# The start of a one-core transformer layer on Trainium2: x on two DMA queues, split first weights, a shared norm, zero-tile matmuls, and the first key begun from x's high parts

## The chip, the core and the metric

The kernel runs on one NeuronCore of a Trainium2 chip. The metric is the device time of one execution in microseconds (us); lower is better. Engine names are those of the profile: PE (TensorE, its matmuls; PEld is its weight load), DVE (VectorE), ACT (ScalarE), POOL (GpSimd), SP (SyncE, which here only starts DMAs).

## What is computed

x has 4 sequences of 256 tokens, 256 features each, in float32. One layer is applied:

```python
x = x + attn(layernorm(x), wq, wk, wv, wo)
x = x + ffn(layernorm(x), W1, W2, W3)
```

The attention has 16 query heads and 4 key/value heads of 128 features, rotary embedding (rope) on queries and keys, and no softmax: the scores are multiplied by a causal decay table of the head. The feed-forward part is `silu(x W1) * (x W3)`, a Walsh-Hadamard transform, and a product with W2.

## The kernel before, in words

**Float32 by three products.** Every operand of a matmul is split into a high part (a copy rounded to the matmul format, made by ACT) and a low part (operand minus high part, made by DVE or POOL). `product` (L272 to L276) issues high x high, high x low and low x high into one PSUM bank. So each operand goes through ACT first, then through DVE or POOL, and then PE may use it.

**Order of the work.** The tokens are done in two halves of 512 (4 tiles of 128 tokens). Each engine has its own hand-written list, and semaphores tie the lists together. `START` (L70) is the first stretch: `X` items transpose the normalised x (two, one for each 128 features), `K`, `Q` and `V` items are projections of 128 columns (K, Q: one head) or of one token tile (V). `LIN` and `LIN_NO` number all such items, `lin_bank` gives their PSUM bank. Then come 16 units `u` (a half and a pair of heads each): `scores` in three parts (`S_FIRST0`, `S_SECOND`, `S_FIRST1`), the decay `mask` by DVE, `high_p` by ACT, `low_p` by DVE, `attend`, `high_o`, `low_o`, `project_out`. Queries and keys are projected two units ahead (`queries`, `key`).

**The first stretch before.** SP loads x of the first half (L246, two DMAs of 256 KB), then three weight chunks of 512 KB (L242): chunk 0 is wk, 1 is the first quarter of wq, 2 is wv, 3 the second quarter of wq, 4 the first of wo. ACT's own queue brings the identity and the rope tables (L561 to L563). There are 3 slots in `w_raw`, so chunk n waits for the low part of chunk n-3. DVE computes the norm's statistics (L724 to L731), POOL the inverse deviation (L640), DVE the normalised x (L748). PE transposes it (L287, eight transposes into banks 0 and 1), ACT takes the high parts (L486), DVE the low ones (L760). Then PE projects K, Q, V, Q, V, ...

**Rope.** For a K or Q item ACT copies the two halves of the bank crosswise into `rope_b` (`swap`, L509 and L510), DVE multiplies by the tables (`rotate`, L779 and L780), POOL adds (`rope_add`, L647), ACT takes the high part (`high_rope`, L515) and POOL the low part (`low_rope`, L654). Two buffers alternate. The first key and the four first queries are called K0, Q0 to Q3 below, the value items V0 to V3, the next queries Q4 and Q5; the second key, K1, is made during unit 1.

**Weights.** `high_weights` (ACT, L481) and `low_weights` (DVE, L754, for chunks 0 to 3; POOL, L659, from chunk 4 on) split a chunk. DVE's list has the low part of chunk 3 after V0 (L865); ACT's list has the high part of chunk 3 before the first `swap` (L569). Unit 0 needs chunk 3 for Q4 and Q5.

**What ends the first stretch on ACT** (L581 to L586): `high_v` of V3, `high_rope` of Q2, `high_p` of the first scores, `high_rope` of Q3, `high_p` of the second scores, `high_weights(4)`, and then unit 0 with the swaps of Q4 and Q5.

Of the kernel before, what the change touches and what calls it, by code (L numbers as in the profile page):

```python
# [57 lines left out]
CHUNKS = [("wk", 0, AT_K), ("wq", 0, AT_Q), ("wv", 0, AT_V), ("wq", 1, AT_Q + CH), ("wo", 0, AT_O),  # L58
# [7 lines left out]
LOW_ON_DVE = 4  # L66
# [3 lines left out]
START = ([("X", 0, k) for k in range(KD)] + [("K", 0, 0), ("Q", 0, 0), ("V", 0, 0), ("Q", 0, 1), ("V", 0, 1),  # L70
          ("Q", 0, 2), ("V", 0, 2), ("Q", 0, 3), ("V", 0, 3)])
# [48 lines left out]
def build(nc, x, wk, wv, wq, wo, w1, w3, w2, cos, sin, decay, ident, hadamard, out):  # L120
    dram = {"wk": wk, "wv": wv, "wq": wq, "wo": wo, "w1": w1, "w3": w3, "w2": w2}

    with ExitStack() as ctx:
# [55 lines left out]
        tables_loaded = sem("tables_loaded")  # L179
# [3 lines left out]
        stored = sem("stored")  # L183
# [5 lines left out]
        half_set, rstd_done, xn_done = sem("half_set"), sem("rstd_done"), sem("xn_done")  # L189
# [47 lines left out]
        def _(sp):  # L237
            def load_chunk(n):
                if n >= SLOTS:
                    wait_low_weights(sp, n - SLOTS)  # L240
                w, i, _ = CHUNKS[n]
                sp.dma_start(w_raw[:, n % SLOTS, :], dram[w][i]).then_inc(w_loaded[n % SLOTS], 16)  # L242

            def load_x(c):
                for i in range(BH * c, BH * (c + 1)):
                    sp.dma_start(x_sb[:, 2 * i:2 * i + 2, :], x[i]).then_inc(x_loaded[i], 16)  # L246
# [5 lines left out]
            for n in range(3):  # L252
                load_chunk(n)
# [4 lines left out]
            load_x(1)  # L258
# [12 lines left out]
        def _(pe):  # L271
# [21 lines left out]
            def project(item):  # L293
# [180 lines left out]
        def _(act):  # L474
            def high_weights(n):
                _, _, at = CHUNKS[n]
                act.wait_ge(w_loaded[n % SLOTS], 16 * (n // SLOTS + 1))
# [159 lines left out]
        def _(pool):  # L637
# [50 lines left out]
            low_rope(("Q", 0, 1))  # L688
            rope_add(("Q", 0, 2))
# [4 lines left out]
            for u in range(UNITS):  # L694
# [12 lines left out]
                if unit_chunk(u) is not None:  # L707
# [7 lines left out]
        def _(dve):  # L715
# [271 lines left out]
```

## Time and profile before

| | |
|---|---|
| median of 3 runs | 277.31 us (277.09, 277.31, 278.17) |
| the profiled execution's own time | 277.34 us |
| its span in the profile | 275.5 us |
| PE busy | 257.6 us (93% of the span) |
| PEld, DVE, ACT, POOL busy | 82%, 75%, 61%, 56% |

The page's second part cuts the span into 40 slices of 6.9 us:

```profile
PE   0796878999999999999999999999999999999995
DVE  2878799899997988967999898795756985144433
ACT  2586787678689767655667777995352552043230
POOL 1049989978878935813597787899709400000000
```

Each digit is the busy share of a slice in tenths. PE is at 9 from the eighth slice on; the first seven slices, up to 48 us, are where it is not.

### The profile page before, as it was taken

To read this page: it belongs to the slowest core of one execution; us is meant where nothing else is said; L and a number is where in the kernel's file an instruction comes from. 1 tells how busy PE (TensorE), PEld (TensorE's weight loads), DVE (VectorE), ACT (ScalarE), POOL (GpSimd) and SP (SyncE) were. 2 spreads that over 40 slices of the span, in tenths; PEclk is the share of its full clock that TensorE was granted. 3 is DMA by queue.
4 is the path that set the end of the run, shared out by engine and by line. 5 is a ranking of instruction groups with operands and counts; after the bars stand their busy time and mean duration, and the time that the engine had idled before them with its cause. 6 is when DMAs were issued, how large, how long until landed. Compare 5 with 4: busy or idle time off the path is not lost.

```text
span 275.5 us, 4150 instructions
## 1 busy us (share of the span) xinstructions
PE 257.6 (93%) x1480; PEld 225.1 (82%) x1480; DVE 206.1 (75%) x324; ACT 167.1 (61%) x279; POOL 153.2 (56%) x111
## 2 busy tenths in 40 slices
PE   0796878999999999999999999999999999999995
PEld 0584766898898988878888888898989879988895
DVE  2878799899997988967999898795756985144433
ACT  2586787678689767655667777995352552043230
POOL 1049989978878935813597787899709400000000
PEclk9999999999999999999999999999999999999999
DMA  7695022102022000000002002200000000200002
GB/s 259 242 355 190 0 80 77 59 20 76 4 76 76 0 2 0 1 4 0 0 2 76 2 0 76 76 4 1 2 0 0 2 0 0 79 0 0 2 0 76
DMA packets 5203, 13.23 MB, mean 48 GB/s; under 512 B 576, under 2 KB 2112, under 8 KB 5184
## 3 DMA queue, kind: packets, MB, share of 16 engines
q1 hardware_dynamic: 4752, 12.65, 13.0%
q10 hardware_dynamic: 432, 0.33, 0.4%
q8 instruction: 12, 0.20, 0.3%
q14 instruction: 7, 0.06, 0.1%
HBM read 11.93 MB, written 1.05 MB: 47 GB/s over the span
## 4 chain that ended last, share of the span: by engine, by line
PE 70%; DVE 13%; POOL 5%; issue 5%; ACT 3%; DMA 3%; SPq 0%; DVEq 0%; POOLq 0%
PE bank L274 24%; PE bank L275 23%; PE bank L276 23%; DVE rope_b L780 3%; POOL qk L647 2%; POOL q_hid L654 2%; DVE rope_a L779 2%; DMA w_raw<-in_wq 1%; DMA x_sb<-in_x 1%; PE bank L287 1%; DVE xn L748 1%; DVE rope_b L817 1%; DVE w_lo L754 1%; POOL w_lo L659 1%; DVE p_lo L798 1%
## 5 line engine op out<-in xcount | busy, mean ns | idle before, releaser
L647 POOL TENSOR_TENSOR qk<-rope_a,rope_b 128x512 f32<-128x512 f32 x40 | 53.5, 1341 | 34.8 <-DVE rope_b L780 34.4
L274 PE MATMUL bank<-xt_hi,w_hi 128*128 128x512 f32 x144 | 57.4, 398 | 1.5 <-DVE rope_a L779 0.8
L275 PE MATMUL bank<-xt_lo,w_hi 128*128 128x512 f32 x144 | 56.9, 395 | 0.0
L276 PE MATMUL bank<-xt_hi,w_lo 128*128 128x512 f32 x144 | 56.6, 393 | 0.0
L654 POOL TENSOR_TENSOR q_hid<-qk,q_hid 128x512 fp32r<-128x512 f32 x32 | 43.0, 1355 | 9.7 <-ACT q_hid L515 9.7
L780 DVE TENSOR_TENSOR rope_b<-rope_b,sin_sb 128x512 f32<-128x512 f32 x40 | 42.1, 1053 | 0.0
L522 ACT ACTIVATE p_hi<-bank 128x512 fp32r<-128x512 f32 x48 | 28.6, 596 | 15.7 <-DVE bank L793 15.2
L779 DVE TENSOR_TENSOR rope_a<-bank,cos_sb 128x512 f32<-128x512 f32 x40 | 27.5, 686 | 14.2 <-ACT rope_b L510 13.5
L275 PE MATMUL bank<-w_lo,o_hi 128*128 128x256 f32 x128 | 36.2, 283 | 0.0
L276 PE MATMUL bank<-w_hi,o_lo 128*128 128x256 f32 x128 | 36.2, 283 | 0.0
L274 PE MATMUL bank<-w_hi,o_hi 128*128 128x256 f32 x128 | 36.1, 282 | 0.0
L274 PEld LDWEIGHTS bank<-xt_hi,w_hi 128*128 128x128 f32 x144 | 27.6, 191 | 8.0 <-DVE rope_a L779 1.0
L798 DVE TENSOR_TENSOR p_lo<-bank,p_hi 128x512 fp32r<-128x512 f32 x48 | 32.7, 680 | 1.4 <-ACT p_hi L522 1.0
L276 PEld LDWEIGHTS bank<-xt_hi,w_lo 128*128 128x128 f32 x144 | 27.5, 191 | 5.9
L793 DVE TENSOR_TENSOR bank<-bank,decay_sb 128x512 f32<-128x512 f32 x48 | 32.0, 688 | 0.5
L275 PEld LDWEIGHTS bank<-xt_lo,w_hi 128*128 128x128 f32 x144 | 27.5, 191 | 5.1
L509 ACT ACTIVATE rope_b<-bank 64x512 f32<-64x512 f32 x40 | 23.8, 596 | 11.8 <-PE bank L276 11.0
L533 ACT ACTIVATE rope_a<-bank 128x512 f32<-128x512 f32 x16 | 9.5, 596 | 28.5 <-PE bank L276 28.5
L803 DVE TENSOR_TENSOR o_lo<-bank,o_hi 128x512 fp32r<-128x512 f32 x32 | 22.0, 687 | 5.9 <-ACT o_hi L526 5.4
L817 DVE TENSOR_TENSOR rope_b<-bank,rope_a 128x512 f32<-128x512 f32 x16 | 11.0, 689 | 20.6 <-ACT rope_a L533 20.6
L526 ACT ACTIVATE o_hi<-bank 128x512 fp32r<-128x512 f32 x32 | 19.1, 596 | 12.1 <-PE bank L276 11.4
L275 PEld LDWEIGHTS bank<-w_lo,o_hi 128*128 128x128 f32 x128 | 24.5, 191 | 0.7
(72 smaller groups left out, 591.4 us busy)
## 6 DMA issues: line engine op xcount, KB each, us to landing
w_raw<-in_w SPq DMA_DIRECT2D x6, 512.0 KB, 3.3
w_raw<-in_wq SPq DMA_DIRECT2D x4, 512.0 KB, 4.8
decay_sb<-in_decay SPq DMA_DIRECT2D x4, 512.0 KB, 6.3
w_raw<-in_wo SPq DMA_DIRECT2D x4, 512.0 KB, 3.2
x_sb<-in_x SPq DMA_DIRECT2D x4, 256.0 KB, 4.5
out<-x_sb SPq DMA_DIRECT2D x8, 128.0 KB, 1.8
w_raw<-in_wk SPq DMA_DIRECT2D x1, 512.0 KB, 4.7
w_raw<-in_wv SPq DMA_DIRECT2D x1, 512.0 KB, 6.6
```

The source lines that it names most:

```text
L274: pe.matmul(o, a_hi, b_hi, start=first, stop=False, skip_group_check=shared)
L275: pe.matmul(o, a_hi, b_lo, start=False, stop=False, skip_group_check=shared)
L276: return pe.matmul(o, a_lo, b_hi, start=False, stop=last, skip_group_check=shared)
L509: act.activation(rope_b[0:h, r % 2, :], lin_bank(n)[h:P], ACT.Copy)
L522: act.activation(p_hi[:, s, :], s_bank[s][:], ACT.Copy).then_inc(p_hi_done, 1)
L647: pool.tensor_tensor(qk[:, r % 2, :], rope_a[:, r % 2, :], rope_b[:, r % 2, :], ALU.add).then_inc(rope_sum, 1)
L654: pool.tensor_tensor(lo, qk[:, r % 2, :], hi.bitcast(F32), ALU.subtract).then_inc(rope_lo, 1)
L779: dve.tensor_tensor(a, src, c, ALU.mult).then_inc(lin_free, 1)
L780: dve.tensor_tensor(b, b, s, ALU.mult).then_inc(rope_parts, 1)
L793: dve.tensor_tensor(src, src, table, ALU.mult).then_inc(mask_done, 1)
L798: dve.tensor_tensor(p_lo[:, s, :], s_bank[s][:], p_hi[:, s, :].bitcast(F32), ALU.subtract).then_inc(p_lo_done, 1)
L803: dve.tensor_tensor(o_lo[:, b, :, :].rearrange("p h t -> p (h t)"), o_bank[:], o_hi[:, b, :, :].rearrange("p h t -> p (h t)").bitcast(F32) ...
```

## The change

Everything is in the first stretch.

- x: sequence 0 stays on SP's queue, sequence 1 goes to ACT's. The identity follows it there; the rope tables move to SP's queue behind chunk 1.
- Chunks: chunk 0 is now wv, chunk 2 is wk. The first 256 columns of wk (head K0) and the first 512 of the first wq chunk (Q0, Q1) are loaded ahead of all chunks by DMAs of their own (`load_first`), split by ACT and DVE (`high_first`, `low_first`) ahead of the rest. The rest of these chunks has 768 and 512 columns.
- Low parts: `LOW_ON_DVE = (0, 3)`; chunks 1 and 2 (their rests) go to POOL.
- Norm: DVE computes the shift, then DVE normalises tiles 0 and 1, ACT tiles 2 and 3.
- PE: 16 matmuls of a zeroed tile by itself (128x512, into bank 7) ahead of the transposes, two behind them. POOL zeroes the tile.
- K0: the four products with x's high parts go first, the two with its low parts last.
- The high part of chunk 3 moves behind V3 in ACT's list, its low part behind Q3 in DVE's list, ahead of the first two masks.

```diff
-CHUNKS = [("wk", 0, AT_K), ("wq", 0, AT_Q), ("wv", 0, AT_V), ("wq", 1, AT_Q + CH), ("wo", 0, AT_O),
+CHUNKS = [("wv", 0, AT_V), ("wq", 0, AT_Q), ("wk", 0, AT_K), ("wq", 1, AT_Q + CH), ("wo", 0, AT_O),
-LOW_ON_DVE = 4
+FIRST = ((2, 0, D), (1, 0, 2 * D))
+FIRST_OF = {n: at for n, _, at in FIRST}
+WARM_FIRST, WARM_NEXT = 16, 2
+LOW_ON_DVE = (0, 3)
@@ block.sync
+            def load_first(i):
+                n, a, b = FIRST[i]
+                w, j, _ = CHUNKS[n]
+                sp.dma_start(w_raw[:, n % SLOTS, a:b], dram[w][j][:, a:b]).then_inc(first_loaded[i], 16)
...
             load_x(0)
-            for n in range(3):
-                load_chunk(n)
+            load_first(0)
+            load_first(1)
+            load_chunk(0)
+            load_chunk(1)
+            sp.dma_start(cos_sb[:], cos).then_inc(tables_loaded, 16)
+            sp.dma_start(sin_sb[:], sin).then_inc(tables_loaded, 16)
+            load_chunk(2)
             load_chunk(3)
@@ block.tensor
+            def warm(times):
+                for _ in range(times):
+                    pe.matmul(bank[7][:], o_hi[:, 0, 0, 0:P], o_hi[:, 0, :, :], start=True, stop=True)
...
+                if item == ("K", 0, 0):
+                    for k in range(KD):
+                        pe.wait_ge(x_hi_done, k + 1)
+                        a = slice(at + k * P, at + (k + 1) * P)
+                        pe.matmul(o[:], w_hi[:, a], xt_hi[:, k, :], start=k == 0, stop=False)
+                        pe.matmul(o[:], w_lo[:, a], xt_hi[:, k, :], start=False, stop=False)
+                    for k in range(KD):
+                        pe.wait_ge(lin_free, LIN_NO[("X", c, k)] + 1)
+                        a = slice(at + k * P, at + (k + 1) * P)
+                        last = pe.matmul(o[:], w_hi[:, a], xt_lo[:, k, :], start=False, stop=k == KD - 1)
+                    last.then_inc(lin_full, 1)
+                    return
...
-            pe.wait_ge(tables_loaded, 48)
-            fill(START)
+            pe.wait_ge(zeroed, 1)
+            warm(WARM_FIRST)
+            pe.wait_ge(ident_loaded, 16)
+            fill(START[:2])
+            warm(WARM_NEXT)
+            fill(START[2:11])
             for u in range(UNITS + 1):
                 if u < UNITS:
                     scores(u, S_FIRST0)
                     scores(u, S_SECOND)
+                if u == 0:
+                    fill(START[11:])
@@ block.scalar
-            act.dma_start(ident_sb[:], ident).then_inc(tables_loaded, 16)
-            act.dma_start(cos_sb[:], cos).then_inc(tables_loaded, 16)
-            act.dma_start(sin_sb[:], sin).then_inc(tables_loaded, 16)
-            high_weights(0)
+            act.dma_start(x_sb[:, 2:4, :], x[1]).then_inc(x_loaded[1], 16)
+            act.dma_start(ident_sb[:], ident).then_inc(ident_loaded, 16)
+            norm_apply(0, range(2, TT))
+            high_first(0)
+            high_first(1)
             high_x(0, 0)
             high_x(0, 1)
+            high_weights(0)
             high_weights(1)
-            high_weights(2)
-            high_weights(3)
...
+            high_weights(2)
             high_v(0, 1)
...
             high_v(0, 3)
-            high_rope(("Q", 0, 2))
+            high_weights(3)
             high_p(0, S_FIRST0)
             high_rope(("Q", 0, 3))
@@ block.gpsimd
             pool.memset(minus_half[:], -0.5).then_inc(half_set, 1)
+            pool.memset(o_hi[:, 0, :, :].bitcast(F32), 0.0).then_inc(zeroed, 1)
             pool.wait_ge(half_set, 1)
             inverse_deviation(0)
+            low_weights(1)
             rope_add(("K", 0, 0))
...
             low_rope(("Q", 0, 1))
+            low_weights(2)
             rope_add(("Q", 0, 2))
@@ block.vector
-            norm_apply(0, range(TT))
-            low_weights(0)
+            norm_shift(0)
+            norm_apply(0, range(2))
+            low_first(0)
+            low_first(1)
             low_x(0, 0)
             low_x(0, 1)
-            low_weights(1)
-            low_weights(2)
-            dve.wait_ge(tables_loaded, 48)
-            fill(START[2:5])
+            low_weights(0)
+            dve.wait_ge(tables_loaded, 32)
+            fill(START[2:10])
             low_weights(3)
-            fill(START[5:])
             mask(0, S_FIRST0)
             mask(0, S_SECOND)
+            fill(START[10:])
```

`START` has 11 items, so PE's `START[11:]` is empty.

How the lists change at two places. First ACT, the end of the first stretch, before (`v_hid` is a value item's high part, `rope_b` a half of a swap, `q_hid` the high part of a query, `p_hi` that of masked scores, `w_hi` a chunk's):

```order
L509 ACTIVATE rope_b<-bank1 64x512
L510 ACTIVATE rope_b<-bank1 64x512
L499 ACTIVATE v_hid<-bank0 128x512
L515 ACTIVATE q_hid<-qk 128x512
L522 ACTIVATE p_hi<-bank2 128x512
L515 ACTIVATE q_hid<-qk 128x512
L522 ACTIVATE p_hi<-bank3 128x512
L481 ACTIVATE w_hi<-w_raw 128x1024
```

and in the change:

```order
L568 ACTIVATE rope_b<-bank1 64x512
L569 ACTIVATE rope_b<-bank1 64x512
L574 ACTIVATE q_hid<-qk 128x512
L558 ACTIVATE v_hid<-bank0 128x512
L539 ACTIVATE w_hi<-w_raw 128x1024
L581 ACTIVATE p_hi<-bank2 128x512
L574 ACTIVATE q_hid<-qk 128x512
L581 ACTIVATE p_hi<-bank3 128x512
L539 ACTIVATE w_hi<-w_raw 128x1024
```

The high part of chunk 3 now stands behind the high parts of Q2 and V3, and ahead of the high part of the first scores and that of Q3.

Second POOL, from the inverse deviation to chunk 4, before (`qk` is a rope sum, `k_lo` and `q_hid` are low parts, `w_lo` is the low part of a chunk):

```order
L640 TENSOR_TENSOR rstd<-var_eps,minus_half 128x4
L647 TENSOR_TENSOR qk<-rope_a,rope_b 128x512 x2
L654 TENSOR_TENSOR k_lo<-qk,k_hi 128x512
L647 TENSOR_TENSOR qk<-rope_a,rope_b 128x512
L654 TENSOR_TENSOR q_hid<-qk,q_hid 128x512 x2
L647 TENSOR_TENSOR qk<-rope_a,rope_b 128x512 x2
L654 TENSOR_TENSOR q_hid<-qk,q_hid 128x512 x2
L659 TENSOR_TENSOR w_lo<-w_raw,w_hi 128x1024
```

and in the change:

```order
L701 TENSOR_TENSOR rstd<-var_eps,minus_half 128x4
L721 TENSOR_TENSOR w_lo<-w_raw,w_hi 128x512
L708 TENSOR_TENSOR qk<-rope_a,rope_b 128x512 x2
L715 TENSOR_TENSOR k_lo<-qk,k_hi 128x512
L708 TENSOR_TENSOR qk<-rope_a,rope_b 128x512
L715 TENSOR_TENSOR q_hid<-qk,q_hid 128x512 x2
L721 TENSOR_TENSOR w_lo<-w_raw,w_hi 128x768
L708 TENSOR_TENSOR qk<-rope_a,rope_b 128x512 x2
L715 TENSOR_TENSOR q_hid<-qk,q_hid 128x512 x2
L721 TENSOR_TENSOR w_lo<-w_raw,w_hi 128x1024
```

A half chunk has come in ahead of the first rope sum, and three quarters of a chunk between the low part of Q1 and the sum of Q2.

## Rows read from the trace of the kernel before

**Rows 1.** The page: busy time of each engine.

```profile
PE 257.6 (93%) x1480; PEld 225.1 (82%) x1480; DVE 206.1 (75%) x324; ACT 167.1 (61%) x279; POOL 153.2 (56%) x111
```

**Rows 2.** Windows: length, busy us (xcount) per engine, PEclk, DMA share, GB/s.

```profile
75.00:100.00 25.00, 25.00 (x156) 22.45 (x155) 21.66 (x34) 20.87 (x37) 18.57 (x14) 1.00 0.12 43
```

**Rows 3.** PE's waits, whole span: us in total, times, longest.

```profile
PE bank L287 <- DVE xn L748: 7.7, 1, 7.7
```

**Rows 4.** Timeline of PE: start us, us, [idle before <-releaser].

```profile
11.11 0.63 PE L275 MATMUL bank<-xt_lo,w_hi 128*128 128x512 f32 x1
...
12.81 0.63 PE L276 MATMUL bank<-xt_hi,w_lo 128*128 128x512 f32 x1
...
25.73 0.50 PE L274 MATMUL bank<-w_hi,xt_hi 128*128 128x512 f32 x1 [2.28 <-DVE v_hid L766]
...
27.00 0.40 PE L276 MATMUL bank<-w_hi,xt_lo 128*128 128x512 f32 x1
...
47.59 0.50 PE L274 MATMUL bank<-q_hid,k_hi 128*128 128x512 f32 x1 [1.34 <-POOL k_lo L654]
```

**Rows 5.** Timeline of DVE and POOL up to the low part of x.

```profile
3.71 0.75 DVE L724 BATCH_NORM_STATS2 stats<-x_sb 128x6 f32<-128x256 f32 x2 [3.71 <-DMA x_sb<-in_x]
4.70 0.75 DVE L724 BATCH_NORM_STATS2 stats<-x_sb 128x6 f32<-128x256 f32 x2 [0.23 <-DMA x_sb<-in_x]
...
6.08 1.02 POOL L640 TENSOR_TENSOR rstd<-var_eps,minus_half 128x4 f32<-128x4 f32 x1 [5.25 <-DVE var_eps L731]
...
10.56 0.69 DVE L760 TENSOR_TENSOR xt_lo<-bank,xt_hi 128x512 fp32r<-128x512 f32 x1 [0.16 <-ACT xt_hi L486]
```

**Rows 6.** Line L737, the norm's shift: ns min/median/max, first and last start.

```profile
L737 DVE SCALAR_TENSOR_TENSOR shift<-mean_var,rstd x2: 261/267/273, 71.9 to 163.5; 128x4 f32<-128x4 f32 x2
```

**Rows 7.** Timeline of ACT.

```profile
13.42 1.06 ACT L481 ACTIVATE w_hi<-w_raw 128x1024 fp32r<-128x1024 f32 x1 [1.00 <-DMA w_raw<-in_wq]
14.50 0.60 ACT L509 ACTIVATE rope_b<-bank 64x512 f32<-64x512 f32 x1
...
29.20 0.63 ACT L515 ACTIVATE q_hid<-qk 128x512 fp32r<-128x512 f32 x1 [1.17 <-POOL qk L647]
...
30.45 0.63 ACT L515 ACTIVATE q_hid<-qk 128x512 fp32r<-128x512 f32 x1
...
31.47 1.05 ACT L481 ACTIVATE w_hi<-w_raw 128x1024 fp32r<-128x1024 f32 x1
32.55 0.59 ACT L509 ACTIVATE rope_b<-bank 64x512 f32<-64x512 f32 x1
...
80.80 2.06 ACT L493 ACTIVATE xn<-x_sb,shift,rstd 128x256 f32<-128x256 f32 x4
```

**Rows 8.** Timeline of POOL.

```profile
17.18 1.30 POOL L647 TENSOR_TENSOR qk<-rope_a,rope_b 128x512 f32<-128x512 f32 x1 [10.08 <-DVE rope_b L780]
19.10 1.29 POOL L647 TENSOR_TENSOR qk<-rope_a,rope_b 128x512 f32<-128x512 f32 x1 [0.63 <-DVE rope_b L780]
...
23.26 1.27 POOL L647 TENSOR_TENSOR qk<-rope_a,rope_b 128x512 f32<-128x512 f32 x1 [0.63 <-DVE rope_b L780]
24.48 2.98 POOL L654 TENSOR_TENSOR q_hid<-qk,q_hid 128x512 fp32r<-128x512 f32 x2
...
32.89 2.38 POOL L659 TENSOR_TENSOR w_lo<-w_raw,w_hi 128x1024 fp32r<-128x1024 f32 x1
35.90 1.30 POOL L647 TENSOR_TENSOR qk<-rope_a,rope_b 128x512 f32<-128x512 f32 x1 [0.63 <-DVE rope_b L780]
```

**Rows 9.** Timeline of DVE, the rope products and a chunk's low part.

```profile
16.42 0.68 DVE L780 TENSOR_TENSOR rope_b<-rope_b,sin_sb 128x512 f32<-128x512 f32 x1
...
17.62 1.40 DVE L780 TENSOR_TENSOR rope_b<-rope_b,sin_sb 128x512 f32<-128x512 f32 x1
...
34.38 1.44 DVE L780 TENSOR_TENSOR rope_b<-rope_b,sin_sb 128x512 f32<-128x512 f32 x1
```

**Rows 10.** Tile w_raw, window 0 to 50 us: the low parts of chunks on DVE.

```profile
L754 DVE TENSOR_TENSOR w_lo<-w_raw,w_hi x4: 1214/1221/1931, 8.4 to 19.5; 128x1024 fp32r<-128x1024 f32 x4
```

**Rows 11.** The page: DMA issues, KB each, us to landing.

```profile
w_raw<-in_wv SPq DMA_DIRECT2D x1, 512.0 KB, 6.6
```

More of the change, by code:

```diff
@@ L65 @@
 FIRST_CHUNKS = 5
-LOW_ON_DVE = 4
-START = ([("X", 0, k) for k in range(KD)] + [("K", 0, 0), ("Q", 0, 0), ("V", 0, 0), ("Q", 0, 1), ("V", 0, 1),
-          ("Q", 0, 2), ("V", 0, 2), ("Q", 0, 3), ("V", 0, 3)])
+FIRST = ((2, 0, D), (1, 0, 2 * D))
+FIRST_OF = {n: at for n, _, at in FIRST}
+WARM_FIRST, WARM_NEXT = 16, 2
+LOW_ON_DVE = (0, 3)
+START = [("X", 0, k) for k in range(KD)] + [("K", 0, 0), ("Q", 0, 0), ("V", 0, 0), ("Q", 0, 1), ("V", 0, 1), ("Q", 0, 2), ("V", 0, 2), ("Q", 0, 3), ("V", 0, 3)]
 def queries(u):
@@ L178, in build @@
         x_loaded = [sem(f"x_loaded{i}") for i in range(NSEQ)]
-        tables_loaded = sem("tables_loaded")
+        ident_loaded, tables_loaded = sem("ident_loaded"), sem("tables_loaded")
+        first_loaded = [sem(f"first_loaded{i}") for i in range(len(FIRST))]
+        first_hi, first_lo = sem("first_hi"), sem("first_lo")
         decay_loaded = [sem(f"decay_loaded{i}") for i in range(4)]
@@ L210, in wait_low_weights @@
         def wait_low_weights(engine, n):
-            if n < LOW_ON_DVE:
-                engine.wait_ge(w_lo_dve, n + 1)
+            on_dve = sum(m <= n for m in LOW_ON_DVE)
+            if n in LOW_ON_DVE:
+                engine.wait_ge(w_lo_dve, on_dve)
             else:
-                engine.wait_ge(w_lo_pool, n + 1 - LOW_ON_DVE)
+                engine.wait_ge(w_lo_pool, n + 1 - on_dve)
         def lin_bank(n):
@@ L241, in load_chunk, with load_x @@
                 w, i, _ = CHUNKS[n]
[L242 to L246, printed above, removed]
+                a = FIRST_OF.get(n, 0)
+                sp.dma_start(w_raw[:, n % SLOTS, a:], dram[w][i][:, a:]).then_inc(w_loaded[n % SLOTS], 16)
+            def load_x(i):
+                sp.dma_start(x_sb[:, 2 * i:2 * i + 2, :], x[i]).then_inc(x_loaded[i], 16)
             def load_decay(i):
@@ L257, in _ @@
             load_decay(1)
[L258 removed]
+            load_x(2)
+            load_x(3)
             load_chunk(5)
@@ L285, in transpose_norm @@
                 for t in range(TT):
-                    pe.wait_ge(xn_done, TT * i + t + 1)
+                    if i == 3:
+                        pe.wait_ge(xn_dve, 2 + t + 1)
+                    elif i == 0 and t < 2:
+                        pe.wait_ge(xn_dve, t + 1)
+                    else:
+                        pe.wait_ge(xn_act, TT * i - 2 + t + 1)
                     last = pe.transpose(dst[:, t * P:(t + 1) * P], xn[:, t, k * P:(k + 1) * P], ident_sb[:])
                 last.then_inc(full, 1)
+            def warm(times):
+                for _ in range(times):
+                    pe.matmul(bank[7][:], o_hi[:, 0, 0, 0:P], o_hi[:, 0, :, :], start=True, stop=True)
             def turn(i, k):
@@ L297, in project @@
                 chunk = ("wk", 0) if kind == "K" else ("wq", h // 4)
-                wait_low_weights(pe, CHUNK_NO[chunk])
+                if h < 2 - (kind == "K"):
+                    pe.wait_ge(first_lo, 1 + (kind == "Q"))
+                else:
+                    wait_low_weights(pe, CHUNK_NO[chunk])
                 at = (AT_K if kind == "K" else AT_Q) + h * KD * P
+                if item == ("K", 0, 0):
[10 more added lines that the diff above has]
+                    return
                 for k in range(KD):
@@ L474, in _, with high_first @@
         def _(act):
+            def high_first(i):
+                n, a, b = FIRST[i]
+                at = CHUNKS[n][2]
+                act.wait_ge(first_loaded[i], 16)
+                act.activation(w_hi[:, at + a:at + b], w_raw[:, n % SLOTS, a:b], ACT.Copy).then_inc(first_hi, 1)
             def high_weights(n):
                 _, _, at = CHUNKS[n]
+                a = FIRST_OF.get(n, 0)
                 act.wait_ge(w_loaded[n % SLOTS], 16 * (n // SLOTS + 1))
@@ L706, in _ @@
                     rope_add(item)
-                if unit_chunk(u) is not None:
+                if unit_chunk(u) is not None and unit_chunk(u) not in LOW_ON_DVE:
                     low_weights(unit_chunk(u))
```

40 lines of the change are left out of this document (26 added, 14 removed).

## The prediction

> **What bounds the kernel now.** I read the page first: PE is busy 257.6 of 275.5 us [rows 1], so 17.9 us are all that any edit off PE can win. The windows say where they lie: from 75 to 100 us PE is busy in every microsecond [rows 2], so the body is PE's and an edit of the start counts by how much earlier or later PE gets there. PE's waits put 7.7 us ahead of the first transpose [rows 3]; its timeline has 2.28 us at 25.73 for a bank that DVE frees, and 1.34 us at 47.59 for the low part of K1 from POOL [rows 4]. From 47.59 on PE waits for nearly nothing. So I ask one question: by how much does the first matmul of unit 2, 47.59 now, move? POOL's timeline shows why it is where it is: POOL starts its first rope sum at 17.18 after 10.08 us of idling, and then works almost without a gap [rows 8]. In the PE rows, K0's matmuls stand (12.81 - 11.11) / 4 = 0.43 us apart, which is 512 columns at 1.2 GHz; those from 25.73 to 27.00 take 1.27 us for five steps, about 0.23 us each after the first, the 2.4 GHz level [rows 4]. So PE starts at the lower of its two clocks.
>
> **The change, to the first rope sum.** Times are from the span's start.
> - x: the two halves land at 3.71 and 4.70, and statistics end 0.75 us after the second, 5.45 [rows 5]. On two queues both share the bandwidth. Bounds: 3.71 + 4 x 0.36 = 5.15 if neither is delayed, 4.70 + 1.43 = 6.13 if both land like the second. I take x0 at 3.9, so 5.35: it is nearer to the row of the first, since only 512 KB have to be moved for both. The inverse deviation then ends at 7.0, where it is 6.08 + 1.02 = 7.10 now [rows 5].
> - Norm: the shift is a new step on the path, 0.27 us [rows 6], to 7.3. ACT needs 0.5 us per tile (four in 2.06) [rows 7]: two tiles from 7.4 to 8.5. DVE's two are done before.
> - ACT's queue now decides: high parts of 256 and 512 columns (about 0.4 and 0.63 us by the 1.06 for 1024 and the 0.63 for 512 [rows 7], 0.1 of each overlapped) stand ahead of the high parts of x, which start at 9.25 and 9.75. High parts of chunk 0 and of the rest of chunk 1 follow, to 11.8. They wait for no DMA: the third weight DMA landed 6.6 us after its issue [rows 11], and only the order of the same bytes changes; the tables' 256 KB behind them are wanted at 13.3.
> - DVE: low parts of 512 weight columns and twice of x (0.69 each) end at 11.35, 11.25 now [rows 5]. PE's first four products of K0 are done by then at either clock level; the last follows, and K0 is complete at about 12.0.
> - Swap of K0: 12.0 instead of 14.50; it waited there for chunk 3's high part (13.42, 1.06 us) [rows 7], which is the edit's real gain. The first rope sum keeps its distance, 17.18 - 14.50 = 2.68: **14.7 instead of 17.18, -2.5 us**.
> - The zero matmuls run while PE idles for 7.7 us anyway [rows 3]: 16 x 0.43 = 6.9 at the worst. Zeroing the tile has no row; bounds are the 0.1 of a tiny memset and the 1.3 of a 512-column POOL operation. At worst the burst ends at 9.0 and the transposes are a little late for ACT at 9.25. They are to bring the 0.23 step to Q0 and the items behind it. POOL's half chunk, 1.3 us, is hidden in the idle 10.08 us [rows 8].
>
> **To the sum of Q2.** Now the second and third sum start 1.92 and 6.08 us after the first [rows 8]. The third waits for swap and rotate of Q1; with ACT's list ahead of it (high part of K0, V0, swap) I get 19.85, 5.15 after the first, since DVE no longer does chunk 3 in between. Then POOL: the sum 1.27, the two low parts 2.98 [rows 8], the new three quarters of a chunk midway between 1.30 and 2.38, 1.85, and the sum of Q2 with a wait for DVE, 1.3 + 0.45. It ends at 27.6; ACT took it at 29.20 before [rows 7]. **-1.6 us: 0.9 of the gain is eaten.**
>
> The 0.45 comes from this: a DVE product with two SBUF inputs takes 0.68 us, but 1.40 and 1.44 when POOL is at work [rows 9], and POOL's pair takes 2.98 instead of 2.6 [rows 8]. The Trainium skill (SBUF — State Buffer, "SBUF: two separate sides") calls this an exclusive lock: the loser blocks until the other's instruction is over. By a sharing of bandwidth instead, the moved three quarters would stretch, not block, and the sum below would be near 278.0; by the lock it is 278.9. The rows 17.62 + 1.40 = 19.02, which is 0.54 after POOL's end at 18.48, are for the lock.
>
> **To unit 2: the new wait.** ACT's list now holds, behind the high part of Q2 (27.65): high part of V3 (28.2), of chunk 3 (28.7 to 29.75). Then DVE makes chunk 3's low part: 1.22 us [rows 10], begun after POOL's low part of Q2 lets go at 30.1, so to 31.2. Behind it on DVE stand both masks, the first over at 31.8. Behind that mask on ACT stand the high parts of the first scores and, at 32.4, of Q3, where it was 30.45 [rows 7]: **+1.95**. POOL waits for Q3 from 30.1 to 33.0, and PE waits for chunk 3 with Q4 from 27 to 31.3. The high part of chunk 4 and the swap of Q4 keep their distances: 34.5 instead of 32.55 [rows 7]. POOL: low part of Q3 to 34.3, chunk 4 from 34.5 (its high part ends then) to 36.9, before 32.89 to 35.27 [rows 8]. DVE's product for Q4 ends 0.55 after it, as 34.38 + 1.44 does now [rows 9]; the sum of Q4 starts at 37.5 instead of 35.90: **+1.6 us**. From there all lists are as before, so the first matmul of unit 2 goes from 47.59 to 49.2, and the end with it.
>
> **Sum.** 277.34 (the profiled execution, 0.03 above the median) - 2.5 + 0.9 + 3.2 (from -1.6 to +1.6) = **278.9 us**. A measurement tells this kernel from no change at about 0.5%, 1.4 us.
>
> **Rivals.**
> - *As summed*: own range 278.2 to 279.8, for ±0.5 of x's landing, hops of 0.1 us, and the K0 stage. Chance 0.56, of which 0.44 above 0.5%.
> - *The waits fall luckily*: statistics end at 5.15, and two of the 0.45 us waits for DVE do not arise (whether they do hangs on tenths). +1.6 - 0.2 - 0.9 = +0.5: 277.8. Chance 0.22.
> - *Faster*: POOL alone sets the pace, ACT's chain stays hidden, and -1.6 us lasts: 275.7. It decides whether chunk 3 and the first mask are through when POOL is ready for the low part of Q3, 30.1. That needs the chain from 27.65 to be 2.5 us long; its rows add up to over 5. The bare shift of -2.5 (274.8) would even need POOL's extra 1.85 hidden. Chance 0.07.
> - *The clock does not hold*: the zero matmuls end by 6.7 to 9, then come short transposes and waits. If K0 to V0 still run at 0.43 instead of 0.23, Q0 is complete some 2 us later and the first sums with it: 280.5. Or the clock falls in the new 4 us wait of PE: Q4 and Q5, 12 matmuls, take 2.4 us more, of which the swap hides most. Rows speak half against it: after 2.28 us of waiting at 25.73 the step was still 0.23 [rows 4], but no row has a wait of 4 us in the body. The Trainium skill (TensorE: Matmul & The Clock Gate, "Why this matters for your kernels") advises against pauses between bursts, because they bring the half clock back; that rule speaks against a burst followed by idling. By it 279.5 to 281.5. Chance 0.15.
> - *An edit without effect*: the slice of PE's list (`START[11:]`) is empty, so scores stay behind V3, as before. Nothing in the sum.
>
> **How the numbers follow.** Slower by over 0.5%: 0.44 + 0.15 = 0.59. Within: 0.12 + 0.22 = 0.34. Faster: 0.07. The predicted time is that of the sum. The range leaves out most of *faster* and the far end of the clock case: 277.3 to 281.0.
>
> **What would show it.** First rope sum near 14.7, and POOL's new chunk ahead of the sum of Q2; PE with a wait of about 4 us that DVE's low part of chunk 3 ends, near 31; ACT's high part of the first scores waiting for the mask; POOL idle some 3 us ahead of the low part of Q3; the first matmul of unit 2 near 49.2. Wrong I would be if the low part of chunk 3 ended before 30, if the K0 step were 0.43, or if unit 2 began at another distance from the sum of Q4 than 11.7 us.

## The result: 0.4% slower, with the first rope sum 2.9 us earlier

| | before | changed |
|---|---|---|
| median | 277.27 us | 278.48 us |
| runs, lowest to highest | 13, beside it on the same chip, 276.83 to 278.17 | 12, 278.32 to 278.63 |
| ratio to before, 95% interval | | 1.0041 [1.0031, 1.0050] |
| profiled execution, its span | 277.34, 275.5 us | 278.35, 276.5 us |

The change costs 1.2 us. That is a loss, since the interval excludes 1, but it is inside the 0.5% that I had set as the bound for "no change". A thirteenth run of the changed kernel took 907.26 us; it is a slow run and is left out.

The page's busy line answers to [rows 1]:

```profile
PE 263.7 (95%) x1498; PEld 229.1 (83%) x1498; DVE 203.8 (74%) x323; ACT 167.6 (61%) x283; POOL 156.3 (57%) x114
```

PE is busier by 6.1 us, though it computes nothing more: the 16 zero matmuls take 6.08 us (below), the two behind the transposes 0.71 us, and the rest is 0.7 us less busy than before. Busy time that computes nothing is why the share alone says little here. Three lines of the view of waits (us in total, times, longest) say more:

```profile
POOL qk L708 <- DVE rope_b L852: 25.2, 25, 5.7
ACT p_hi L581 <- DVE bank L865: 17.3, 11, 2.1
POOL q_hid L715 <- ACT q_hid L574: 12.6, 7, 4.4
```

In before's same view these three stood at 34.4, 15.2 and 9.7 us. POOL's wait for DVE ahead of the first rope sum went from 10.08 to 0.87 us (it waits another 4.66 us ahead of its half chunk, for ACT's high part), and 2.1 us and 2.9 us came back in the other two, as ACT waiting for a mask and POOL waiting for a high part. The timelines show both. First ACT, against [rows 7] (start us, us, operation, in brackets the idle time before it and what ended it):

```profile
8.96 1.06 ACT L544 ACTIVATE xt_hi<-bank 128x512 fp32r<-128x512 f32 x2
...
11.57 0.60 ACT L568 ACTIVATE rope_b<-bank 64x512 f32<-64x512 f32 x1
...
27.06 0.63 ACT L574 ACTIVATE q_hid<-qk 128x512 fp32r<-128x512 f32 x1 [3.68 <-POOL qk L708]
27.59 0.58 ACT L558 ACTIVATE v_hid<-bank 128x512 fp32r<-128x512 f32 x1
28.07 1.05 ACT L539 ACTIVATE w_hi<-w_raw 128x1024 fp32r<-128x1024 f32 x1
31.23 0.60 ACT L581 ACTIVATE p_hi<-bank 128x512 fp32r<-128x512 f32 x1 [2.11 <-DVE bank L865]
31.72 0.62 ACT L574 ACTIVATE q_hid<-qk 128x512 fp32r<-128x512 f32 x1
...
33.81 0.60 ACT L568 ACTIVATE rope_b<-bank 64x512 f32<-64x512 f32 x1
```

ACT swaps K0 at 11.57 (14.50 before) and makes Q2's high part at 27.06 (29.20), but Q3's at 31.72 (30.45). So the lead of 2.1 us turns into a lag of 1.3 us between Q2 and Q3 in its list: between them stand chunk 3's high part at 28.07 and a 2.11 us wait for the mask. DVE:

```profile
3.85 1.41 DVE L789 BATCH_NORM_STATS2 stats<-x_sb 128x6 f32<-128x256 f32 x4 [3.85 <-DMA x_sb<-in_x]
...
6.94 0.16 DVE L802 SCALAR_TENSOR_TENSOR shift<-mean_var,rstd 128x4 f32<-128x4 f32 x1 [1.20 <-POOL rstd L701]
...
29.15 1.43 DVE L826 TENSOR_TENSOR w_lo<-w_raw,w_hi 128x1024 fp32r<-128x1024 f32 x1 [3.27 <-ACT w_hi L539]
30.51 1.28 DVE L865 TENSOR_TENSOR bank<-bank,decay_sb 128x512 f32<-128x512 f32 x2
...
35.65 1.14 DVE L852 TENSOR_TENSOR rope_b<-rope_b,sin_sb 128x512 f32<-128x512 f32 x1
```

DVE idles 3.27 us for ACT's high part of chunk 3, then makes the low part, and only then the masks. POOL, against [rows 5, 8]:

```profile
5.89 1.02 POOL L701 TENSOR_TENSOR rstd<-var_eps,minus_half 128x4 f32<-128x4 f32 x1 [4.60 <-DVE var_eps L796]
...
14.24 1.29 POOL L708 TENSOR_TENSOR qk<-rope_a,rope_b 128x512 f32<-128x512 f32 x1 [0.87 <-DVE rope_b L852]
...
23.52 1.81 POOL L721 TENSOR_TENSOR w_lo<-w_raw,w_hi 128x768 fp32r<-128x768 f32 x1
25.30 2.98 POOL L708 TENSOR_TENSOR qk<-rope_a,rope_b 128x512 f32<-128x512 f32 x2
28.24 1.26 POOL L715 TENSOR_TENSOR q_hid<-qk,q_hid 128x512 fp32r<-128x512 f32 x1
32.42 1.30 POOL L715 TENSOR_TENSOR q_hid<-qk,q_hid 128x512 fp32r<-128x512 f32 x1 [2.92 <-ACT q_hid L574]
33.86 2.38 POOL L721 TENSOR_TENSOR w_lo<-w_raw,w_hi 128x1024 fp32r<-128x1024 f32 x1
36.87 1.30 POOL L708 TENSOR_TENSOR qk<-rope_a,rope_b 128x512 f32<-128x512 f32 x1 [0.63 <-DVE rope_b L852]
```

The sum of Q4 stands at 36.87 (35.90 before), +0.97. PE, against [rows 4]:

```profile
1.34 6.08 PE L318 MATMUL bank<-o_hi 128*128 128x512 f32 x16 [1.34 <-POOL o_hi L743]
...
23.08 0.80 PE L295 MATMUL bank<-w_hi,xt_hi 128*128 128x512 f32 x1 [2.01 <-DVE v_hid L838]
...
30.68 0.47 PE L295 MATMUL bank<-xt_hi,w_hi 128*128 128x512 f32 x1 [2.30 <-issue]
...
48.58 0.50 PE L295 MATMUL bank<-q_hid,k_hi 128*128 128x512 f32 x1 [1.35 <-POOL k_lo L715]
```

For the product of Q4 at 30.68 the profile names no releaser ("issue" is time in which it shows nothing that the engine waited for); DVE's low part of chunk 3, which PE's list waits for there, ended 0.10 us before it. Unit 2 begins at 48.58 instead of 47.59, +0.99, and the span is longer by 1.0: what happens up to there is paid one to one.

### The profile page after: what moved, and what is told of

It reads as the page before. It is cut to its first block, busy times and chain, and to the rows that moved or that the text cites. A ratio compares the mean times of both kernels' runs of the same rounds, so it can differ in the third digit from the quotient of the medians.

```text
span 276.5 us, 4195 instructions
## 1 busy us (share of the span) xinstructions
PE 263.7 (95%) x1498; PEld 229.1 (83%) x1498; DVE 203.8 (74%) x323; ACT 167.6 (61%) x283; POOL 156.3 (57%) x114
## 4 chain that ended last, share of the span: by engine, by line
PE 71%; DVE 11%; POOL 6%; issue 5%; ACT 5%; DMA 1%; DVEq 0%; POOLq 0%
PE bank L295 24%; PE bank L296 23%; PE bank L297 23%; POOL qk L708 2%; DVE rope_b L852 2%; POOL q_hid L715 2%; DVE rope_a L851 1%; DMA x_sb<-in_x 1%; PE bank L313 1%; DVE stats L789 1%; DVE rope_b L889 1%; POOL w_lo L721 1%; DVE p_lo L870 1%; DVE bank L865 1%; ACT w_hi L539 1%
## 5 line engine op out<-in xcount | busy, mean ns | idle before, releaser
L295 PE MATMUL bank<-xt_hi,w_hi 128*128 128x512 f32 x142 | 55.9, 394 | 3.1 <-issue 2.3
L296 PE MATMUL bank<-xt_lo,w_hi 128*128 128x512 f32 x142 | 55.5, 391 | 0.0
L297 PE MATMUL bank<-xt_hi,w_lo 128*128 128x512 f32 x142 | 55.3, 389 | 0.0
L295 PEld LDWEIGHTS bank<-xt_hi,w_hi 128*128 128x128 f32 x142 | 26.7, 188 | 9.8 <-issue 2.9
L297 PEld LDWEIGHTS bank<-xt_hi,w_lo 128*128 128x128 f32 x142 | 26.7, 188 | 5.7
L296 PEld LDWEIGHTS bank<-xt_lo,w_hi 128*128 128x128 f32 x142 | 26.7, 188 | 4.9
L721 POOL TENSOR_TENSOR w_lo<-w_raw,w_hi 128x1024 fp32r<-128x1024 f32 (+2 forms) x12 | 27.7, 2308 | 4.8 <-ACT w_hi L539 4.7
```

Of the source, the lines that this page charges most:

```text
L295: pe.matmul(o, a_hi, b_hi, start=first, stop=False, skip_group_check=shared)
L296: pe.matmul(o, a_hi, b_lo, start=False, stop=False, skip_group_check=shared)
L297: return pe.matmul(o, a_lo, b_hi, start=False, stop=last, skip_group_check=shared)
L721: pool.tensor_tensor(w_lo[:, at + a:at + CH], w_raw[:, n % SLOTS, a:], w_hi[:, at + a:at + CH].bitcast(F32), ALU.subtract).then_inc(w_lo_p ...
```

## The experiments

All are measured against the kernel before. "First sum" is the start of POOL's first rope sum. The transfer of x lands up to 0.3 us apart from run to run (the inverse deviation starts between 5.86 and 6.15), so the last column takes that start off.

| kernel | median us | ratio to before [95%] | first sum | from inverse deviation to first sum |
|---|---|---|---|---|
| before | 277.3 to 277.5 | 1 | 17.18 | 11.10 |
| changed | 278.48 | 1.0041 [1.0031, 1.0050] | 14.24 | 8.35 |
| chunk 3's high part early | 276.38 | 0.9956 [0.9940, 0.9971] | 14.47 | 8.37 |
| rest of wk late on POOL | 278.69 | 1.0039 [1.0025, 1.0053] | 14.34 | 8.36 |
| both moved | 275.83 | 0.9940 [0.9924, 0.9956] | 14.30 | 8.36 |
| no zero matmuls | 279.51 | 1.0065 [1.0050, 1.0081] | 14.82 | 8.67 |
| before + zero matmuls | 277.49 | 1.0000 [0.9987, 1.0014] | 17.12 | 11.02 |
| key in the usual order | 279.07 | 1.0049 [1.0034, 1.0064] | 14.98 | 8.96 |
| norm all on DVE | 278.22 | 1.0025 [1.0015, 1.0035] | 14.10 | 8.10 |
| x on one queue | 278.35 | 1.0027 [1.0017, 1.0037] | 14.21 | 8.35 |
| filler in the changed kernel | 278.49 | 1.0035 [1.0023, 1.0046] | 14.41 | 8.36 |
| both moved + filler | 275.70 | 0.9932 [0.9917, 0.9947] | 14.45 | 8.36 |
| and norm on DVE | 275.41 | 0.9922 [0.9908, 0.9936] | 13.97 | 8.11 |
| and chunk 4's low part on DVE | 274.90 | 0.9911 [0.9894, 0.9927] | 14.19 | 8.11 |

### Chunk 3's high part early

My theory was that one place in ACT's list turns the gain into a loss.

```diff
             swap(("Q", 0, 3))
+            high_weights(3)
             high_rope(("Q", 0, 2))
             high_v(0, 3)
-            high_weights(3)
```

> The changed kernel, with one line of ACT's list moved: the high part of chunk 3 stands behind the swap of Q3 instead of behind V3. Theory (the mask chain is the new wait): DVE makes chunk 3's low part at about 26 to 28 instead of 29.15 to 30.58, the high part of Q3 follows its sum near 29.5 instead of 31.72, the first matmul of unit 2 goes from 48.58 to about 46.4, time 278.5 - 2.2 = 276.3 us, faster than the kernel before. Rival (POOL's moved weights alone cost the gain): nothing changes, 278.4 us.

Measured 276.38, 2.1 us less than the changed kernel, where 276.3 was expected. DVE and POOL in its timelines:

```profile
26.03 2.30 DVE L826 TENSOR_TENSOR w_lo<-w_raw,w_hi 128x1024 fp32r<-128x1024 f32 x1
```

```profile
25.52 3.96 POOL L708 TENSOR_TENSOR qk<-rope_a,rope_b 128x512 f32<-128x512 f32 x2
29.44 2.55 POOL L715 TENSOR_TENSOR q_hid<-qk,q_hid 128x512 fp32r<-128x512 f32 x2
...
34.95 1.30 POOL L708 TENSOR_TENSOR qk<-rope_a,rope_b 128x512 f32<-128x512 f32 x1 [0.62 <-DVE rope_b L852]
```

The low part now starts at 26.03, in DVE's former idle time. POOL no longer waits between the low parts of Q2 and Q3, and the sum of Q4 is 1.92 us earlier. It could have been more: beside POOL's sums the low part took 2.30 us, not 1.22.

### The rest of wk late on POOL

This is the rival: the 1.81 us of new work on POOL ahead of the sum of Q2 might be the cost by themselves.

```diff
             low_rope(("Q", 0, 1))
-            low_weights(2)
...
             low_rope(("Q", 0, 3))
+            low_weights(2)
             low_weights(4)
```

> The changed kernel, with POOL's low part of the rest of wk behind the low part of Q3 instead of ahead of the sum of Q2. Theory (mask chain): the sum of Q2 ends 1.8 us earlier, but chunk 3's high part still waits for V3, and POOL has to do the same work later, ahead of the low part of chunk 4: 278.4 us, no gain. Rival (POOL's 1.85 us in that place are the loss): 276.6 us.

Measured 278.69. POOL's and DVE's timelines:

```profile
23.60 1.30 POOL L708 TENSOR_TENSOR qk<-rope_a,rope_b 128x512 f32<-128x512 f32 x1
...
30.97 1.29 POOL L715 TENSOR_TENSOR q_hid<-qk,q_hid 128x512 fp32r<-128x512 f32 x1 [2.92 <-ACT q_hid L574]
32.21 4.21 POOL L721 TENSOR_TENSOR w_lo<-w_raw,w_hi 128x768 fp32r<-128x768 f32 x2
37.05 1.28 POOL L708 TENSOR_TENSOR qk<-rope_a,rope_b 128x512 f32<-128x512 f32 x1 [0.63 <-DVE rope_b L852]
```

```profile
34.19 2.78 DVE L852 TENSOR_TENSOR rope_b<-rope_b,sin_sb 128x512 f32<-128x512 f32 x1
```

The sum of Q2 comes 1.70 us earlier, and the low part of Q3 with it, 1.45 us earlier, after the same wait of 2.92 us for Q3's high part. That lead is then spent: the moved 768 columns stand with chunk 4's in 4.21 us ahead of the sum of Q4, and DVE's second product for Q4 takes 2.78 us beside the second of them. So the work costs as much in the new place, and moving it wins nothing. The run does not show that POOL's load costs nothing, because it is still there ahead of the sum of Q4; a kernel with this work off POOL and chunk 3's high part late was not run. What the place in ACT's list costs, 2.1 us, is what the experiment above shows.

### Both moved

```diff
-LOW_ON_DVE = (0, 3)
+LOW_ON_DVE = (0, 2, 3)
...
-            low_weights(2)
...
-            fill(START[2:10])
+            fill(START[2:7])
+            low_weights(2)
+            fill(START[7:10])
```

The line that leaves is POOL's; the rest of the diff is in DVE's list, and chunk 3's high part is early here too.

> The changed kernel with the high part of chunk 3 behind the swap of Q3, and the low part of the rest of wk made by DVE between V1 and Q2 (DVE has gaps there) instead of by POOL. Theory: 278.5 - 2.9 = 275.6 us, with the first matmul of unit 2 at about 45.7, 0.7 less than with the first edit alone. Rival (DVE and POOL block each other as much as is moved): the same as with the first edit alone, 276.3 us.

Measured 275.83, a gain of 1.6 us over before (277.46 beside it). With chunk 3's high part early, taking the 1.81 us off POOL is worth 0.55 us.

### No zero matmuls

```diff
-WARM_FIRST, WARM_NEXT = 16, 2
+WARM_FIRST, WARM_NEXT = 0, 0
```

> The changed kernel without the 18 matmuls of the zeroed tile. Theory (the burst brings the higher clock to K0 and Q0): K0's matmuls stand 0.43 us apart until about 13, the first rope sum goes from 14.24 to about 15.2, and all of it reaches the end: 279.5 us. Rival (ACT's list ahead of the swap decides, the clock does not): first rope sum within 0.3 us of 14.24, 278.6 us.

Measured 279.51: the zero matmuls earn about 1.0 us by the medians (0.7 by the ratios). The time is the one expected, but the place is not: in the profile only 0.32 us of it is seen at the first sum by the last column (0.58 us with x's landing), where 1.0 was expected. Where the rest arises stays open: that execution, 278.91, is the quickest of the six, and the others (279.27 to 279.68) left no trace. In the trace K0's steps are 0.56, 0.43 and 0.32 us, and 0.23 from 11.25 on:

```profile
9.94 0.77 PE L337 MATMUL bank<-xt_hi,w_hi 128*128 128x512 f32 x1
10.50 0.63 PE L338 MATMUL bank<-xt_hi,w_lo 128*128 128x512 f32 x1
10.93 0.48 PE L337 MATMUL bank<-xt_hi,w_hi 128*128 128x512 f32 x1
11.25 0.39 PE L338 MATMUL bank<-xt_hi,w_lo 128*128 128x512 f32 x1
```

### The zero matmuls alone, on the kernel before

```diff
             pool.memset(minus_half[:], -0.5).then_inc(half_set, 1)
+            pool.memset(o_hi[:, 0, :, :].bitcast(F32), 0.0).then_inc(zeroed, 1)
...
+            pe.wait_ge(zeroed, 1)
+            for _ in range(16):
+                pe.matmul(bank[7][:], o_hi[:, 0, 0, 0:P], o_hi[:, 0, :, :], start=True, stop=True)
             pe.wait_ge(tables_loaded, 48)
```

> The kernel before with the zero burst alone (16 matmuls of the cleared o_hi into bank 7 at the program's start, nothing else changed). Theory: the first key's product gets faster (its steps in row 4 at 11.11 to 12.81 stood at 0.43, now 0.23, so it ends about 1 us earlier, near 12), but ACT's swap of it stands at 14.50 behind w_hi of two chunks whose last one waits for wv (rows 7, 11), so the first sum of the rope stays at 17.2 +-0.1 and the time stays: 277.3, ratio 1.000 +-0.001. Rival, that the burst is worth in any surroundings what it gave in the changed kernel (0.6 us at the first sum): 276.4 to 276.8, first sum at 16.6.

Measured 277.49, ratio 1.0000. K0's last matmul starts at 11.65 instead of 12.81, but ACT's list hides all of it (the DMA that it waits for is that of chunk 3, from wq, and not wv as I had written):

```profile
13.37 1.06 ACT L484 ACTIVATE w_hi<-w_raw 128x1024 fp32r<-128x1024 f32 x1 [1.44 <-DMA w_raw<-in_wq]
14.45 0.59 ACT L512 ACTIVATE rope_b<-bank 64x512 f32<-64x512 f32 x1
```

A faster PE is worth nothing while ACT waits for a DMA ahead of the swap. In this trace it even costs a little later. PE is through with V2 sooner, so its wait for the bank of V3 grows from 2.28 us [rows 4] to 3.55, and the product behind it runs at the 0.43 step (granted clock 0.66 from 25 to 30 us, 1.00 in before):

```profile
25.66 0.79 PE L274 MATMUL bank<-w_hi,xt_hi 128*128 128x512 f32 x1 [3.55 <-DVE v_hid L770]
```

The first mask starts at 29.86 instead of 28.67 and unit 2 at 47.91 instead of 47.59. These 0.3 us stand in one trace (its own time is 277.63); the medians do not show them.

### The other parts of the front

K0 in the usual order (the branch for `("K", 0, 0)` in `project` deleted):

> The changed kernel with the first key's product in the usual order (it waits for both low parts of x; three matmuls for each k). Theory: the product, which starts at 9.68 and ends near 11.5, then starts when the first low part of x is there, near 10.35, and ends near 12.0; the first sum goes from 14.24 to about 14.7, and all up to the first matmul of unit 2 (48.58) moves with it, so 278.9, ratio to before 1.006. Rival, that low parts of x bound the product's end in either order: nothing, 278.5.

Measured 279.07, +0.6. The first sum is 0.61 us later, more than the 0.46 expected: the product starts at 10.65, 0.15 us after the first of x's two low parts (10.35 was expected, and x landed 0.13 us later in this trace).

The whole first norm on DVE:

```diff
-            norm_shift(0)
-            norm_apply(0, range(2))
+            norm_apply(0, range(TT))
```

with ACT's `norm_apply(0, ...)` deleted and the waits' counts adapted.

> The changed kernel with all four tiles of the first norm on DVE, no shift for it, and ACT free to make w_hi of the first head's pieces early. Theory: four tiles on DVE end at about 6.95+1.38=8.3, the last of ACT's ended at 8.23, so the transposes end within 0.1 us of where they did; sharing the norm bought nothing: 278.5 +-0.2, first sum 14.24 +-0.15. Rival, that the sharing was worth half of DVE's 1.38 us: 279.0, first sum 14.7.

Measured 278.22, just under the 278.3 to 278.7 expected and a little better than with the sharing (-0.25 us at the first sum, -0.26 us in the medians). DVE's four tiles take 1.38 us; two tiles, a shift, a hop and two tiles on ACT are no shorter, and they keep ACT from the first weights.

x on one queue (SP issues both halves):

> The changed kernel with both first pieces of x issued by SP, one behind the other, as before. Theory: the last two stats start at 4.70 and end at 5.35 instead of 5.26 (before's own rows), and the first pieces of the weights land 0.6 us later without being waited for: first sum within 0.15 us of 14.24, time 278.5 to 278.7. Rival, that the second queue is worth what its issue takes (0.6 us): 279.1.

Measured 278.35; the same 8.35 us to the first sum. That column counts from behind x's landing and so cannot price a queue, but the inverse deviation itself starts at 5.86 here and at 5.89 in the changed kernel. The second queue bought nothing: DVE's statistics ran without a gap here too, from 3.76 (3.85 in the changed kernel). The gap of [rows 5] is in the trace of before with the zero matmuls as well (second start at 4.71), so it seems to come with the whole chunk that stands behind x there; that was not tried by itself.

### Keeping PE busy through its wait

In the changed kernel PE fell to the 1.2 GHz step after the wait at 23.08. Eight zero matmuls into bank 5 fill that wait (twelve in the kernel with both moved, where it is 2.97 us):

```diff
-            fill(START[2:11])
+            fill(START[2:10])
+            pe.wait_ge(lin_free, LIN_NO[("Q", 0, 1)] + 1)
+            for _ in range(8):
+                pe.matmul(bank[5][:], o_hi[:, 0, 0, 0:P], o_hi[:, 0, :, :], start=True, stop=True)
+            fill(START[10:11])
```

> The changed kernel with eight more zero matmuls (into bank 5, free by then) in PE's wait before the values of the fourth tile, so that PE works from 21.07 to about 22.9 and the product at 23.08 starts without a pause. Theory: the step there stays at 0.23 (it was 0.43 from 23.08 to 25.81), the scores end 1.4 us earlier, near 27.0, and nobody waits for them (the masks wait for DVE's low part of chunk 3, at 30.51): 278.5, nothing. Rival, that the slower clock there is one of the terms that ate the front's gain: 277.6 or less.

Measured 278.49 where the changed kernel has 278.48; the step held at 0.23 (granted clock 1.00 from 20 to 25 us, 0.81 without). So the slow clock there was free. The scores were through sooner, the wait ahead of Q4 grew from 2.30 to 3.88 us, and Q4 began at the 0.43 step instead (granted clock 0.66 from 30 to 35 us); that cost nothing measurable either.

> The kernel with both pieces of work moved (275.83) with twelve zero matmuls in the same wait of PE, which is 2.97 us there. There DVE waits 0.53 us for the scores before the masks (28.04), and ACT 0.58 us for the values of the fourth tile, both behind a product in 0.43 steps. Theory: those waits go, masks start near 27.5, all behind moves 0.5 us: 275.3, ratio 0.992. Rival, that masks are then held by DVE's low part of chunk 3 (which ends at 27.5 already) or POOL's sums in full: no more than 0.1 us, 275.7.

Measured 275.70, a gain of 0.13 where 0.5 was expected. The masks did start earlier (27.59 instead of 28.04), and the rotation of Q4 with them (32.17 instead of 32.59). But POOL's low part of chunk 4 started only 0.12 us earlier, and the second product, which ends 0.55 us behind it in both kernels, took 1.44 us instead of 1.15. I had followed the chain to the mask and not on to the next collision.

### The best version

> The last one with the whole first norm on DVE as well. Theory: that run's gain in the changed kernel, 0.13 us in the trace's span at the first sum and 0.26 us in the time, adds up: 275.1 where the last one gives 275.3. Rival: the front is no longer what bounds it, 275.3.

Measured 275.41, 0.29 us less than the last: this gain adds up. Last, the collision was removed by giving chunk 4's low part to DVE:

```diff
-LOW_ON_DVE = (0, 2, 3)
+LOW_ON_DVE = (0, 2, 3, 4)
...
-            low_weights(4)
...
                 mask(u, S_FIRST1)
+                if u == 0:
+                    low_weights(4)
```

> The last kernel (275.41) with the low part of chunk 4 moved from POOL (30.84, 2.39 us, beside DVE's rotation of Q4, whose second product took 1.44 us against it) to DVE, where it stands behind the first mask of unit 0 in a wait of 0.87 us that DVE has there. Theory: it takes about 1.2 us alone on DVE, so the rotation of Q4 starts 0.35 us later, its second product is back at 0.7 us (0.75 us less), and so are those of Q5; the sum of Q4 comes 0.3 to 0.4 us earlier, and the time with it: 275.0. Rival, that DVE is by then the bound and every piece on it is paid in full: the sum of Q4 0.35 us later, 275.7.

Measured 274.90, 0.9% under before and 3.6 us under the changed kernel. DVE's timeline:

```profile
30.99 1.21 DVE L827 TENSOR_TENSOR w_lo<-w_raw,w_hi 128x1024 fp32r<-128x1024 f32 x1
32.13 0.68 DVE L852 TENSOR_TENSOR rope_a<-bank,cos_sb 128x512 f32<-128x512 f32 x1
32.73 0.67 DVE L853 TENSOR_TENSOR rope_b<-rope_b,sin_sb 128x512 f32<-128x512 f32 x1
```

1.21 us instead of POOL's 2.39, and the product behind it 0.67 instead of 1.44. The sum of Q4 starts at 33.48, 0.37 us earlier than in the last kernel, though x landed 0.22 us later in this trace.

## Why the prediction held, and where it was off

**The forecast.** 278.9 us with its own range from 278.2; measured 278.48. The case *as summed* is the one that came; it landed on the near side of the 0.5% bound, where I had seen it with 0.12 against 0.44 beyond, so the class that I called likeliest (slower by over 0.5%, 0.59) did not come. The sum said +1.6, the span says +1.0. Stage by stage the sum is off by -0.46 (to the first rope sum), -0.13 (to Q2's high part), -0.04 (to the sum of Q4) and nothing behind it: all to one side, so no error covers another.

**To the first rope sum: under-sized.** I had 14.7 and -2.5; it was 14.24 and -2.9. Of the 2.94 us, 0.19 are x's earlier landing in this trace. The lead over my sum grows along the path by small terms, each of which I had too dear: statistics end at 5.26 (I had 5.35); the shift took 0.16 us, not the 0.27 of [rows 6], which come from the body; ACT's high parts of x start at 8.96 (9.25); and K0 was complete at 11.5, not 12.0. The distance from swap to sum is the 2.67 that I carried over. Of the causes, the key's new order is worth 0.6, the zero matmuls 0.3 at the first sum and more in the time, the second queue nothing, the shared norm -0.25. By subtraction, and if the parts add up, the rest, about 2 us, belongs to the first pieces of the weights and to chunk 3's high part leaving the head of ACT's list; that was not run by itself, though the zero matmuls on the kernel before show that nothing on PE could get past it. POOL's half chunk took 1.81 us and not 1.3, but ended at 13.37, hidden ahead of the first sum as I had it.

**To Q2's high part: right.** 12.82 us behind the first sum where I had 12.95. The term for the three quarters of a chunk, 1.85 by interpolation, measured 1.81. This stretch hangs on what POOL and DVE cost each other. The Trainium skill (SBUF — State Buffer, "SBUF: two separate sides") has the exclusive lock, and the runs are for it: a low part of 1024 columns takes 1.21 to 1.22 us alone and 2.30 beside POOL's sums, and a product that takes 0.67 us alone is held until POOL's instruction is over. DVE's second product for Q4 took 1.14 us in the changed kernel, 1.44 in before [rows 9] and 2.78 with the rest of wk late, and it ended 0.55 us after POOL's low part of chunk 4 each time (36.79 behind 36.24, 35.82 behind 35.27, 36.97 behind 36.42). Sharing evenly could at most double the 0.67 us, to 1.34. The 278.0 that I gave for a mere sharing of bandwidth was not reached, but with the front 0.5 us off, the time alone would not have told the two apart; the rows do.

**The new wait: right, in place and size.** From Q2's high part to the sum of Q4 I had 9.85 us, and it took 9.81. DVE's low part of chunk 3 ends at 30.58 (I had 31.2), POOL idles 2.92 us. Moving one line of ACT's list gives 2.1 us back, which shows the cause of the new wait. The load on POOL ahead of the sum of Q2 is the other term that ate the gain, as summed; moving it (278.69) does not price it. PE's wait ahead of Q4 was 2.30 us, not 4: scores that I had expected done by 27 ran until 28.4, because V3's product ahead of them was at the lower clock; where the clock held (the filler in the changed kernel) the wait was 3.88.

**From the sum of Q4 on: right.** 11.71 us to unit 2, 11.7 predicted, and nothing is given or taken behind it.

**The clock case.** The step held at 0.23 from K0 on, so the front's part of that rival is refuted. Its other part happened in another place, after 2.01 us of waiting at 23.08, and cost nothing, because the masks waited for chunk 3 anyway. The Trainium skill (TensorE: Matmul & The Clock Gate, "Why this matters for your kernels") warns of pauses between bursts. The traces agree that a pause can bring the lower level back, and here one of 2.01 us already did, which is shorter than those that the page warns of. What it costs was 0 in the changed kernel, 0.1 us in the one with both pieces moved, and 0.3 us in the trace of before with the zero matmuls.

## What to carry to other kernels

Making a start faster only moves work up to the first place in a queue that is written for the old times; read on from there, engine by engine, what stands ahead of the next item that somebody waits for. A split piece that is moved later to clear the front has to be put back at the next idle time of its consumer, not at the end of the list. And when two engines hold each other up, price a move by which instruction it will lie beside: 1.2 us of work was 2.3 in one place and 1.2 in the next.

## What was not expected of the hardware

**The clock after short waits is not a matter of the wait's length alone.** The norm-on-DVE kernel waits 2.04 us at the same place where the changed kernel waited 2.01, and keeps its step; later, after 3.85 us, all twelve matmuls of Q4 and Q5 run at the lower level (the first two are shown):

```profile
22.93 0.50 PE L295 MATMUL bank<-w_hi,xt_hi 128*128 128x512 f32 x1 [2.04 <-DVE v_hid L837]
23.26 0.39 PE L296 MATMUL bank<-w_lo,xt_hi 128*128 128x512 f32 x1
...
30.53 0.76 PE L295 MATMUL bank<-xt_hi,w_hi 128*128 128x512 f32 x1 [3.85 <-issue]
31.09 0.63 PE L296 MATMUL bank<-xt_lo,w_hi 128*128 128x512 f32 x1
```

The changed kernel fell at 23.08 and not at 30.68, after 2.30 us. The fall can also come later than the first matmul. The kernel with chunk 3's high part early waits 1.99 us, begins at the higher level and is at the 0.43 step from the third matmul on (granted clock 0.87 from 20 to 25 us, 0.79 from 25 to 30):

```profile
23.29 0.50 PE L295 MATMUL bank<-w_hi,xt_hi 128*128 128x512 f32 x1 [1.99 <-DVE v_hid L838]
23.63 0.54 PE L296 MATMUL bank<-w_lo,xt_hi 128*128 128x512 f32 x1
23.96 0.63 PE L297 MATMUL bank<-w_hi,xt_lo 128*128 128x512 f32 x1
```

Ahead of V3, waits of 1.96, 2.02, 2.04 and before's 2.28 [rows 4] were followed by 0.23 steps only; those of 1.99 (twice) and 2.00 by 0.43 steps from the third, sixth and seventh matmul on; those of 2.01, 2.97 and 3.55 by 0.43 from the start. Ahead of Q4, 2.30 held, 2.31 (twice) gave 0.43 steps from the third and the fourth matmul on, and 2.33 from the start. What decides between them is left open.

**The profile's granted clock does not show the slow start.** It reads 1.00 from 5 to 15 us in before, where K0's steps are 0.43 us [rows 4]; there the level has to be read from the steps.

**Zeroing a tile is cheap on POOL.** The 128x512 clear took 0.53 us, where I had bounds of 0.1 and 1.3; nothing hung on it.

**Without the zero matmuls the clock still rises early in the one execution that was traced.** The 0.23 step is reached at 11.25, while in before 12.81 still ran at 0.43 [rows 4]. The runs without them also spread more (278.91 to 279.68, against 278.32 to 278.63). That the burst narrows the spread is not shown: on the kernel before, the runs with it lie between 277.13 and 278.80, those without between 276.87 and 278.45.
